# First attention layer: lead of four units, maxima turned inside the step, values in three places, token copy on GpSimd

## What is computed

```python
xn = _layernorm(x)
qkv = xn @ w_qkv + b_qkv
scores = jnp.einsum('bhtd,bhsd->bhts', q, k) / np.sqrt(D_HEAD)
scores = scores + _rpe_bias(T, w1_rpe, b1_rpe, w2_rpe, b2_rpe)[None]
attn = jax.nn.softmax(scores, axis=-1)
out = jnp.einsum('bhts,bhsd->bhtd', attn, v)
s = out.reshape(B, T, C) @ w_out + b_out
g = silu(experts(xn))          # top 2 of 8
x = x + s * g
```

## Time and profile before

| | us |
|---|---|
| median of 3 runs | 998.69 |
| lowest, highest | 994.81, 999.81 |
| the profiled execution | 1001.72 |
| its span, first to last instruction | 999.9 |
| busy: PE, DVE, ACT, POOL | 786.2, 645.5, 509.3, 411.4 |

### The profile page before, as it was taken

One profiled execution on the slowest core, in us unless ns is written; L12 is line 12 of the kernel. 1 busy time (PEld: TensorE's weight loads), 2 busy tenths in 40 slices (PEclk: granted clock), 3 DMA queues, 4 the chain that ended last, 5 costly groups with the idle time before them and its releaser, 6 DMA issues.

```text
span 999.9 us, 19881 instructions
## 1 busy us (share of the span) xinstructions
PE 786.2 (79%) x6259; PEld 506.5 (51%) x6278; DVE 645.5 (65%) x1137; ACT 509.3 (51%) x883; POOL 411.4 (41%) x394
## 2 busy tenths in 40 slices
PE   0894787989988998854999999525598898989984
PEld 0652444555554554422555555314476666666663
DVE  6552786887788778832655655366356767676763
ACT  1243254676677766642433433258365555555542
POOL 7006776554555454421777777673210101010000
PEclk9996899999999999986999999856799999999997
DMA  5595745444544453142212222240665646464621
GB/s 141 194 192 138 174 121 123 97 94 102 123 115 92 100 122 88 31 136 59 58 53 53 58 55 54 78 122 16 142 135 124 148 117 159 115 157 117 136 58 51
DMA packets 132671, 106.13 MB, mean 106 GB/s; under 512 B 23317, under 2 KB 124633, under 8 KB 129545
## 3 DMA queue, kind: packets, MB, share of 16 engines
q1 hardware_dynamic: 122348, 91.23, 39.8%
q0 software_dynamic: 4352, 8.99, 2.9%
q10 hardware_dynamic: 5920, 5.24, 1.7%
HBM read 54.60 MB, written 50.03 MB: 105 GB/s over the span
## 4 chain that ended last, share of the span: by engine, by line
PE 27%; DMA 10%; DVE 7%; issue 4%; ACT 4%; SPq 2%; POOL 1%; DVEq 0%; ACTq 0%; POOLq 0%
PE ps L671 8%; DMA od_d<-ev 5%; PE ps L692 3%; PE ps L1567 3%; DVE mx L1272 3%; DMA rec<-od_d 2%; PE ps L683 2%; PE ps L665 2%; PE ps L1576 1%; ACT rows L893 1%; PE ps L673 1%; PE ps L1519 1%; SPq L1113 1%; PE ps L1517 1%; PE ps L1545 1%
## 5 line engine op out<-in xcount | busy, mean ns | idle before, releaser
L1272 DVE TENSOR_REDUCE mx<-ps 128x4 f32<-128x1024 f32 (+1 forms) x224 | 268.4, 1212 | 146.8 <-PE ps L1513 69.9
L1423 ACT ACTIVATE probs<-probs 128x1024 f32<-128x1024 f32 x128 | 131.8, 1051 | 64.9 <-DVE probs L1282 63.6
L1428 ACT ACTIVATE probs<-ps 128x1024 f32<-128x1024 f32 x96 | 96.8, 1024 | 82.9 <-PE ps L1545 55.8
L1202 POOL TENSOR_TENSOR qkr<-qkf,qk 128x512 f32<-128x512 f32 x27 | 31.3, 1160 | 244.0 <-ACT qk L1392 238.4
L1230 POOL TENSOR_TENSOR probs<-probs,tabB 128x1024 f32<-128x1024 f32 x42 | 99.5, 2369 | 74.6 <-ACT probs L1435 74.6
L1511 PE MATMUL ps<-tabA,eyeb 128*128 128x512 bf16 x256 | 102.3, 399 | 25.9 <-DMA ks<-parts_d 10.9
L1567 PE MATMUL ps<-probs,vpad 128*32 128x256 f32 (+1 forms) x2048 | 118.7, 362 | 4.2 <-ACT probs L1423 3.6
L1282 DVE TENSOR_TENSOR probs<-ps,tabB 128x1024 f32<-128x1024 f32 x86 | 101.5, 1210 | 4.3 <-PE ps L1539 4.3
L1513 PE MATMUL ps<-ks,qs 96*128 96x256 bf16 x512 | 102.3, 282 | 0.0
L1539 PE MATMUL ps<-qs,ks 99*128 99x256 bf16 x512 | 77.2, 280 | 6.8 <-DMA qs<-mT 2.6
L671 PE MATMUL ps<-qs,probs 128*128 x144 | 80.9, 644 | 1.4
(11 more groups left out here) (226 smaller groups left out, 1530.1 us busy)
## 6 DMA issues: line engine op xcount, KB each, us to landing
parts_d<-qk SPq DMA_DIRECT2D x64, 192.0 KB, 4.3
qs<-parts_d SPq DMA_DIRECT2D x32, 384.0 KB, 5.0
ks<-parts_d SPq DMA_DIRECT2D x32, 384.0 KB, 6.7
parts_d<-qk SPq DMA_DIRECT2D x64, 128.0 KB, 3.2
od_d<-ev SPq DMA_DIRECT2D x64, 128.0 KB
slots_in<-probs SPq DMA_DIRECT2D x1, 4680.0 KB
probs<-slots_in SPq DMA_DIRECT2D x72, 65.0 KB, 1.8
parts_d<-qk SPq DMA_DIRECT2D x64, 64.0 KB, 1.9
```

Of the source, the lines that this page charges most:

```text
L1272: nc.vector.tensor_reduce(mx[:, s.buf(), t, heads[0]:heads[-1] + 1], ring[:, slot].rearrange("p (h n) -> p h n", n=w), AX.X, ALU.max).then ...
L1423: nc.scalar.activation(probs[:, j, :], probs[:, j, :], ACT.Exp).then_inc(exp_done, 1)
L1428: nc.scalar.activation(probs[:, j, :], ring[:, slot], ACT.Exp).then_inc(exp_done, 1)
```

## The change

In layer 0 alone (layer 1 gets its old numbers from the same tables): A leads B by four units instead of three; the late value groups of batch k-2 are three pairs (2,3 before A3, 4,5 before B1, 6,7 before B2), and only 0,1 stay in the step of their B units; the maxima are split and turned inside the step, before B6, and copied by ScalarE after exponential 4; units 0, 2, 3 instead of 0, 2, 4 go by ScalarE and GpSimd; QK stands before A3, V before A4, the reciprocal at the end of the step; SP issues all three parts first and the inverses last; and the token copy is GpSimd's first work in each step.

```diff
-        self.order = [("A", 0), ("A", 1), ("A", 2)]
-        for j in range(count - 3):
-            self.order += [("B", j), ("A", j + 3)]
+        self.order = [("A", j) for j in range(lead)]
+        for j in range(count - lead):
+            self.order += [("B", j), ("A", j + lead)]
...
-    U = Units(8 if layer == 0 else 6)
+    U = Units(8, 4) if layer == 0 else Units(6, 3)
...
-    LATE = 2 if layer else 4
-    SCALE = 2 if layer else 0
-    INVERT = 7 if layer else 10
-    VALUES = {9: (0, 1)} if layer else {13: (0, 1), 15: (2, 3)}
-    ASIDE = () if layer else (0, 2, 4)
-    ORDER = tuple(range(NU)) if layer else (1, 0, 3, 2, 5, 6, 4, 7)
-    PROJECT = 10 if layer else 8
+    LATE = {0: (2, 3, 4, 5)} if layer else {3: (2, 3), 6: (4, 5), 8: (6, 7)}
+    VALUES = {9: (0, 1)} if layer else {12: (0, 1)}
+    SCALE, INVERT, PROJECT = (2, 7, 10) if layer else (7, 15, 10)
+    QK, V, TURN = (1, 4, NU * 2) if layer else (3, 5, 14)
+    ASIDE = () if layer else (0, 2, 3)
+    ORDER = tuple(range(NU)) if layer else (1, 0, 2, 4, 5, 6, 3, 7)
+    A_PART, A_OUT, A_TWO, A_VAL, A_MAX = (2, 0, 4, 4, NU * 2) if layer else (4, 7, 5, 5, 12)
...
+                if layer == 0:
+                    if s.has(2):
+                        parts(s, 0)
+                        parts(s, 1)
+                        parts(s, 2)
+                    if s.has(-2):
+                        outputs_out(s)
+                        sums_in(s)
+                        outputs_in(s)
+                    if s.has():
+                        maxima(s)
+                    if s.has(-2):
+                        inverses_out(s)
+                        inverses_in(s)
...
+            def tokens(s):
+
+                if s.has(-1):
+                    pool.wait_ge(v_full, s.n(-1) + 1)
+                nc.gpsimd.tensor_copy(xb[:], xnT[:, bass.ds(s.n() * T, T)]).then_inc(xb_done, 1)
+
             def body(s):
+                if s.has() and layer == 0:
+                    tokens(s)
                 if s.has(2) and (layer or s.k >= HELP):
                     rest_one(pool, nc.gpsimd, s)
                 for n, j in enumerate(apart(s.k)):
                     if n == 1 and s.has(2):
                         rest_two(pool, nc.gpsimd, s)
+                    if n == 2 and s.has():
+                        parts_gpsimd(pool, s)
                     if s.has(-1):
                         bias_aside(pool, s, n, j)
...
-                if s.has():
+                if layer and s.has():
                     if s.has(-1):
                         act.wait_ge(v_full, s.n(-1) + 1)
                     nc.scalar.activation(xb[:], xnT[:, bass.ds(s.n() * T, T)], ACT.Copy).then_inc(xb_done, 1)
...
+                    if pos == A_MAX and s.has():
+                        max_rows(s)
...
+                    if pos == TURN and s.has():
+                        turn_maxima(s)
```

More of the change, by code:

```diff
@@ L959, with __init__ @@
 class Units:
[L963 removed]
+    def __init__(self, count, lead):
         self.count = count
[L965 to L968 removed]
+        self.order = [("A", j) for j in range(lead)]
+        for j in range(count - lead):
+            self.order += [("B", j), ("A", j + lead)]
+        self.order += [("B", j) for j in range(count - lead, count)]
     def exists(self, k, kind):
@@ L1257, in body @@
                     rest_two(pool, nc.gpsimd, s)
-                if layer == 0 and s.has() and s.k >= HELP:
-                    parts_gpsimd(pool, s)
             if layer:
@@ L1453, in body @@
                 for pos, (kind, j) in enumerate(U.order):
-                    if pos == (0 if layer else 4) and s.has(-2):
+                    if pos == A_PART and s.has(2):
+                        parts_one(s)
+                    if pos == A_OUT and s.has(-2):
                         outputs(s)
                     if kind == "B" and U.exists(s.k, kind):
-                        if j in apart(s.k):
-                            take(s, j, U.slot(s.k, pos))
-                        else:
-                            exponential(s, j, U.slot(s.k, pos))
-                        if apart(s.k) and j in (2, 4, 6):
-                            exponential(s, j - 2, 0)
-                    if pos == 1 and s.has(2):
-                        parts_one(s)
-                    if pos == 4 and s.has(2):
+                        for what, i in (SEQ[j] if apart(s.k) else (("exp", j),)):
+                            if what == "take":
+                                take(s, i, U.slot(s.k, pos))
+                            else:
+                                exponential(s, i, U.slot(s.k, pos))
+                    if pos == A_TWO and s.has(2):
                         parts_two(s)
-                    if pos == 4 and s.has():
+                    if pos == A_VAL and s.has():
                         values(s)
+                    if pos == A_MAX and s.has():
+                        max_rows(s)
                 if layer and s.has(-3):
@@ L1474, in body @@
                     act.dma_start(v.wdn, v.down_w.rearrange("e (c i) h -> i e c h", c=2)).then_inc(v.w_load, 16)
-                if s.has():
+                if A_MAX >= len(U.order) and s.has():
                     max_rows(s)
@@ L1577, in projections, with turn_maxima @@
                 mm.then_inc(qk_full, 1)
+            def turn_maxima(s):
+                misc_free(pe, s, "M")
+                pe.wait_ge(max_parts, 4 * (s.n() + 1))
+                nc.tensor.transpose(misc[0:PARTS * 2 * H, 0:P // 2].bitcast(BF16),
+                                    m3[:].rearrange("p c h t -> p (c h t)"), eyeb[:]).then_inc(mt_full, 1)
             def body(s):
-                def late_values(first, last):
+                for pos, (kind, j) in enumerate(U.order):
                     if s.has(-2):
-                        for j in range(first, last):
-                            values(s, -2, j)
-                if layer:
-                    late_values(LATE, NU)
-                for pos, (kind, j) in enumerate(U.order):
-                    if layer == 0 and pos in (1, 3):
-                        late_values(pos + 3, pos + 5)
-                    if pos == 1 and s.has(2):
+                        for i in LATE.get(pos, ()):
+                            values(s, -2, i)
+                    if pos == QK and s.has(2):
                         projections(s)
-                    if pos == 4 and s.has():
+                    if pos == V and s.has():
                         misc_free(pe, s, "V")
@@ L1620, in body @@
                             values(s, -1, i)
-                if s.has():
-                    misc_free(pe, s, "M")
-                    pe.wait_ge(max_parts, 4 * (s.n() + 1))
-                    nc.tensor.transpose(misc[0:PARTS * 2 * H, 0:P // 2].bitcast(BF16),
-                                        m3[:].rearrange("p c h t -> p (c h t)"), eyeb[:]).then_inc(mt_full, 1)
+                if TURN >= len(U.order) and s.has():
+                    turn_maxima(s)
             if layer:
```

41 lines of the change are left out of this document (21 added, 20 removed).

## The result

| | before | after |
|---|---|---|
| median of 4 runs | 999.00 | 1034.61 |
| lowest, highest | 994.81, 999.81 | 1031.03, 1035.36 |
| the profiled execution | 1001.72 | 1034.16 |
| its span | 999.9 | 1031.8 |

The changed kernel is slower: 1.0358 times the time of before, 95% interval 1.032 to 1.0396. The forecast was 1027 with a range of 1017 to 1044, so the median lies 7.6 above it. Step by step the changed kernel is the faster one over most of the stage; one wait of 64 us outweighs that.

What follows compares the result with a forecast made beforehand. No engine was full; the step was a loop of waits. Terms 66.6 - 0.7 - 3.0 - 20.3 - 8.2 - 4.6 (steps 14, 15) - 2.0 = +27.8 gave 1029.5 profiled, 1027 us as median, range 1017 to 1044.

Steps and rivals of the forecast that it cites:

- the stall: Layer 0, step 0: V waits for GpSimd's token copy behind all 64 scatters, +66.6 us, ends 66.3 and 71.2.
- Restart, steps 0 and 1: V of step 0 to first maximum of step 2, TensorE restarting at low clock: 34.0 us against 34.7, -0.7.
- Step 2: Third step of layer 0: VectorE's work plus one stall of 0.65 before m3, 21.1 us against 24.1, -3.0.
- Steady steps: Steps 4 to 13 of layer 0: 18.0 us each instead of 20.03, -20.3 in all.
- The walk: One steady step followed operation by operation from b5, using durations from the trace of before; it gives 18.0 us.
- sign of 2.4 us: Expected in the trace of after: VectorE idle before maxima near 2.4 us per steady step, instead of 4.0.
- Rival 1: Steps 3 to 15 gain nothing and stay near 20 us, giving 1054 us; chance 0.12.
- both thin covers: Steady step: transpose hidden ahead of B6 by 0.07 us, GpSimd's bias add before the split in time by 0.02.
- Step 3: Step 3 of layer 0, 26.2 us with its scatter wait and TensorE's restart, becomes a steady step: -8.2.
- Tail: End of layer 0: B0 of step 16 loses its 2.10 wait for the maxima's transfer; -2, give or take 3.
- Rival 2: TensorE becomes the bound of the steps at 16.5 us each, giving 1007 us; chance 0.05.
- Rival 3: Step 0's stall is short, scatters running faster while attention stands still; 0.72 us each breaks even, not slower; chance 0.03.

## Why the prediction was right, and where its terms were off

The mechanism is the forecast's: one stall from the copy's place in the queue, and a gain in every step behind it. Four terms failed, and the total hides them in part: the stall came below its own lower end, the low clock at the start of step 1 was in the sum and did not come, the low clock in steps 2 and 3 was not in the sum and came, and in step 16 a wait that the forecast had ended was followed by another.

**The stall.** Forecast +66.6 with 66.3 as the lower end; it came to +62.9, below that end. The copy took 0.40 (0.5 taken) and the landing 1.39 (1.64 taken). Most of the rest is no mechanism: in this execution of after all of the stage began 2.5 earlier (first maximum of step 0 at 94.38 instead of 96.86), and the scatters' last issue with it, at 160.56 instead of 163.86. With the copy's edit alone V stands at 166.09 and the first maximum of step 0 at 97.56, a shift of 65.6 from the earlier trace rows. The sum took the place of the scatters from one execution as if it were fixed, and the last issue lies between 159.3 and 164.3 in the profiled executions; taken from the first maximum of step 0, the shift is 65.4 in after and 64.9 with the copy alone. The scatters from first to last issue took 83.0 in before and 82.3 in after. The choice of the shorter landing over 5.57 was right. The Trainium skill (GPSIMD Engine Reference, 3.1 and 4.1) gave some 0.4 us for the copy; the trace agrees, with 0.40.

**Restart, steps 0 and 1.** Forecast -0.7, measured -3.4. The restart at the low clock came as said, at V, and was over at 168.52. What failed is the next term, the first stretch of step 1 of some 5 us in which TensorE at the low clock feeds VectorE. The forecast's 34.0 are 9 to the transpose and 20.2 of work in step 1, which leaves 4.8 for that stretch. Measured are 9.76 to the transpose, 1.20 from there to the first maximum of step 1, and 20.30 for the step. From 173.20 to 179.00, behind the transpose, the granted clock is 1.00; in before it was at 0.50 behind the transpose at 110.08, and the three parts were 9.56, 2.05 and 23.09. With the copy alone (the stall and the old order) they are 10.65, 1.20 and 21.52, again with the clock at 1.00 behind the transpose; with the new order and no stall 7.96, 1.91 and 21.44. So the stall, by the clock behind it, and the new order both shorten this stretch. Against the copy alone after has 2.1 less: 0.9 before the first maximum of step 1, where one A unit fewer stands behind V, which the forecast had counted, and 1.2 in step 1, where VectorE no longer waits twice 0.5.

**Step 2.** Forecast -3.0, measured -0.3. The sum counted VectorE's work and one stall, and left TensorE's clock out. Three windows, steps 1, 2 and 3 of after (start:end, length, busy times, granted clock), and VectorE's timeline in step 2:

```profile
174.42:194.72 20.30, 15.48 (x106) 8.92 (x105) 20.15 (x22) 9.74 (x14) 0.40 (x1) 0.94 0.41 84
194.72:218.54 23.82, 20.54 (x155) 11.08 (x154) 20.60 (x25) 11.53 (x18) 0.40 (x1) 0.86 0.36 83
218.54:237.87 19.33, 18.50 (x163) 11.32 (x162) 16.77 (x18) 13.10 (x19) 10.64 (x10) 0.98 0.51 112
```

```profile
196.30 1.22 DVE L1297 TENSOR_REDUCE mx<-ps 128x4 f32<-128x1024 f32 x1 [0.36 <-PE ps L1539]
198.01 1.23 DVE L1297 TENSOR_REDUCE mx<-ps 128x4 f32<-128x1024 f32 x1 [0.48 <-PE ps L1539]
201.47 1.23 DVE L1297 TENSOR_REDUCE mx<-ps 128x4 f32<-128x1024 f32 x1 [2.24 <-PE ps L1539]
```

Step 1 has one pair of value groups where a steady step has four, so TensorE is busy 15.48 of its 20.30, and at its end it waits 1.08, 0.38 and 0.61 for VectorE; it begins step 2 at the low level. VectorE waits 0.36 and 0.48 for A units of 1.7, and 2.24 before m3, where the forecast had 0.65, because the value products ahead of it take 1.53 instead of 1.00 and began late. The run with TensorE kept busy had this step at 21.75 against the 21.1 of the forecast, with a wait of 1.21 before m3 and none before m1 and m2. That shows the cause; at the high level the forecast was 0.65 short.

**Steady steps.** Forecast 18.0 with 17.4 to 19.2 around it, measured 18.25. The walk holds: VectorE's stalls before m3 and m4, walked at 0.53 and 0.63, are 0.49 and 0.56 in the trace, and m7 is at 16.02 behind b5 instead of 15.74. The mis-sized term is the A unit that has value products behind it, twice in that run, 0.97 from start to start instead of 0.88; the products V and Y add 0.09 together. The forecast's sign of 2.4 us of VectorE's idle time before maxima a step did not come: it is 1.2, and 0.35 before adds, because the scaling takes 1.2 instead of 0.41 and fills what the walk had as waits. That also takes the 0.7 by which, walked on with the forecast's durations, m5's slot was free before B3: here B3 starts (303.48) just when m5 is done (302.22 + 1.21). One more reading against the text: the transpose does wait,

```profile
307.61 0.26 PE L1609 MATMUL ps<-eyeb,m 128*96 128x128 bf16 x1 [0.65 <-POOL m L1239]
```

but VectorE's four adds from b4 to b7 follow without a gap, so the cover that the forecast called 0.07 thin held, and the wait costs nothing. Rival 1 had it that both thin covers give way together, and no run shows that. The nearest is the run with the maxima turned at the end, where B6 and B7 are not held but A0 is: 20.6 a step.

**Step 3.** Forecast -8.2, measured -6.8: 19.3 instead of 18.0, with the clock at 0.98 in it. The other second is the low clock once more: TensorE begins this step at the low level too, its 512-column product takes 0.63 until 218.76 and 0.38 from 219.56, and VectorE waits 1.46 before m3, where it waits 0.49 in a steady step:

```profile
223.57 1.23 DVE L1297 TENSOR_REDUCE mx<-ps 128x4 f32<-128x1024 f32 x1 [1.46 <-PE ps L1539]
```

The mechanism is shown by the run with the copy back on ScalarE, where this step keeps its wait for the scatters and takes 25.6.

**Tail.** Forecast -4.3 with step 15, measured -1.8. B0 of step 16 has no wait for the maxima's transfer any more, as the forecast said; but its term named no wait that follows, and there is one. Timeline of TensorE in step 16 of after, the answer to the earlier trace rows:

```profile
455.64 1.08 PE L1593 MATMUL ps<-probs,vpad 128*32 128x256 f32 x8 [2.35 <-ACT probs L1448]
456.65 1.03 PE L1565 MATMUL ps<-qs,ks 99*128 99x256 bf16 x4
```

Step 16 has no A units and no QK, so the late value group of unit 3 comes at once and waits 2.35 for its exponential, in place of the 2.10, and B0 behind it takes 1.03 for four products instead of 0.61: from 455.60 to 462.00 the granted clock is 0.51, where the first B units of before ran at 1.00 (428 to 432). So the term failed by a wait that it had not looked for and by the clock behind it.

**The rivals.** Rival 2 (TensorE bound, 16.5 a step) is out: no version came below 18.2 a step on average. Rival 3 needed the scatters every 0.72 in the stall. They went on at 0.97 + 0.30 through the 64 us in which VectorE stood still. The forecast held this to speak against the rule of the Trainium skill (SBUF — State Buffer, Who interferes with whom). It doesn't: the same section counts among what holds the shared ports neither a reduction nor a VectorE operation with at most one input in SBUF outside the 2-port modes. In before, of the 56 us that VectorE was busy between 95 and 165, 50 were maxima and adds out of PSUM. So by the rule there was next to nothing to gain from an idle VectorE, and no run here tests it.

**The sum.** The gains together came to 32.2 instead of 38.8, the stall to 3.7 less than forecast, and the rest to 1.2 more: the two profiled executions agree with the sum to 4 us because two misses partly cancel, which is luck. The median is off by 7.6, as the forecast took the profiled execution of after to lie 3 over its median, like before's, and it lay 0.5 under it. The range had room for that.

## What to carry to other kernels

An operation moved to an idle-looking engine stands behind everything already on that engine's queue: look for the last thing ahead of its first instance, not at the engine's busy share. Here 0.4 us of copying cost 57 us in step 0 and again 3.9 us when it began one step too early; with the copy left on ScalarE the same change is 2.4% faster than before, and with all of GpSimd's help kept back until the scatters have landed 2.6%. And a wait of TensorE at a step's end can cost twice, since it may return at the lower clock: take such waits away before tuning positions.

## What was not expected of the hardware

**A VectorE operation beside a GpSimd one.** The scaling (two inputs from SBUF, 128 x 256) took 0.41 in before and takes 1.16 here. Timelines of VectorE and GpSimd in after:

```profile
301.13 1.16 DVE L1323 TENSOR_TENSOR on<-raw,rden 128x256 f32<-128x256 f32 x1
```

```profile
300.85 1.16 POOL L1224 TENSOR_TENSOR qk<-qkr,qk 128x512 bf16<-128x512 f32 x1
```

GpSimd had begun 0.28 earlier, and the scaling ends 0.28 after it (302.29 and 302.01). That it was made to wait for GpSimd's operation agrees with the rule of the Trainium skill (SBUF — State Buffer, Who interferes with whom) that a VectorE operation with two inputs in SBUF and a GpSimd operation that reads SBUF share ports and the one that comes first holds them; moved away it took 0.42. VectorE's adds out of PSUM beside GpSimd's adds kept their 1.22.

**The clock after short waits.** With the maxima turned at the end, waits of 1.6 to 1.8 for TensorE at the end of a step were followed by the low level (1.2 GHz, granted clock 0.50) in eight of ten steady steps and not in the other two. With the lead of three, waits of 1.8 to 2.0 ahead of B6 were followed by it in three of ten, and before's waits of 0.93 to 1.04 at the step's end in none of the steady steps. What decides between them no run shows. The ten runs with the maxima turned at the end spread over 10 us, the four of each other kernel over 1 to 6; that the clock makes the spread is likely and was not shown.

**The start of the stage.** The first maximum of step 0 lay between 92.9 and 97.6 in the profiled executions, behind a setup that is the same code in all kernels. Differences of 3 us between medians, as between kernels here (971.57, 972.41, 974.07, 975.95), are not told from this by the time alone; the steps in the trace are.
